# Three-layer decoder block on one core: another order of fills between self-attention and cross-attention, cross-attention two steps sooner, and three waits moved in the feed-forward part

## The chip, the cores and the metric

The kernel runs on one core of one Trainium2 chip. The metric is the device time of one execution in microseconds (us), the median of three runs. The engines are called by their names in the profile: TensorE is PE (its weight loads PEld), VectorE is DVE, ScalarE is ACT, GpSimd is POOL, SyncE, which only issues DMAs here, is SP.

## What is computed

The reference is a post-norm decoder block on x of 8 x 128 x 512 in float32. Its core:

```python
x = layernorm(x + attn(x))      # 32 heads of 16, causal, biases, projections 512 x 512
x = layernorm(x + xattn(x, ctx, ctx, mask))
    # q: 512 -> 32 heads of 128 with rope; k, v: 512 -> 8 heads of 128, k with rope; 4 query heads per kv head
    # out = softmax(q k^T / sqrt(128)) v, then 4096 -> 512
x = layernorm(x + ffn(x))       # gate, up: 512 -> 1376, silu(gate) * up, down: 1376 -> 512
    # their weights are 4-bit codes with a scale and a zero per group of 128 rows
```

Products of float32 are made of float16 halves: a value is split into hi and lo, and each product takes three matmuls (hi x hi, hi x lo, lo x hi). So nearly every tensor is written twice after it leaves a PSUM bank, the hi half by ScalarE (a copy), the lo half by VectorE (value less hi), or both by GpSimd.

## The kernel before, in words

**One list of steps.** The program is one sequence of steps t. Steps 0 to 63 (STEPS1 = 64) are the tiles of the first attention, then a few without attention, and from T0 = 72 on 64 steps v = t - T0 of the cross-attention, until END = 136, and seven more. Every engine walks the same list of steps in its own program with its own order of work within a step, and engines wait for one another through semaphores that count finished tiles. Nothing else orders them.

**First attention, a step t.** TensorE: scores1(t), a projection's part or a fill, weigh1(t - 3) (probabilities by values), turn1(t - 1) (transposes of the probabilities), in every second step turn_out1. VectorE: row_max1(t) (nmax), p1_lo(t - 2) (pT), in every second step normalise, in every eighth turned_out (oTh, oTl). ScalarE: exps1(t) (ebias, prob), p1_hi(t - 1) (pT).

**Fills.** fill_plan (line 61) lists, by hand, extra work of TensorE and the step in which it runs: "o" b, the first attention's output projection of batch b; "t" (0, b), four transposes of its layer norm's result for batch b; "k", "v" and "q" (n, h), projections of the cross-attention's block n (a pair of kv head g and half of the batches, in ORDER). Twelve matmuls of 512 columns make an "o", "k", "q"; 48 of 128 columns a "v". Fill f writes bank f % 2, so it waits until fill f - 2 has been taken out of it (fill_free). Who takes it out (consume, on VectorE): of "k" and "q" rotation_parts (rcos, rsin), then GpSimd's rotation_sum (rot), ScalarE's rotated_hi and GpSimd's rotated_lo one step later; of "v" and "t" ScalarE's values_hi or turned_hi (aTh) and VectorE's values_lo or turned_lo (aTl); of "o" VectorE's add_self and statistics (res, lnst, lnmv), then GpSimd's inverse_sd (lnve, lnrs), and one step later VectorE's apply_norms (res), after which "t" may be made. The first "q" of a half of the batches waits for the four turned tiles of that half. TensorE runs the first fill of a step ahead of weigh, the others behind it.

**Weight splits.** weight_plan (line 123) gives the steps at which the cross-attention's weights of head g are split: QKV_SLOT six pieces, OUT_SLOT four. Those of g = 0 run on GpSimd (split_piece, three instructions), the rest on ScalarE (hi) and, one step later, VectorE (lo). SP loads the next head's weights when the last were split, in program order with its other DMAs.

**Cross-attention, a step v.** TensorE: scores(v), first fill, weigh(v - 2), other fills, merge(v - 3) (output projection into bank 6 or 7). VectorE: add_out(v - 4), row_max(v) (nmax), a weight piece, apply_norms, the first fill if it is "k" or "q", row_sum_inverse(v) (rden), the first fill otherwise, o_lo(v - 2), the other fills. ScalarE: p_hi(v - 1), the first fill's rotated_hi, exps(v), other rotations, weight pieces, o_hi(v - 2), then "v" and "t". GpSimd: p_lo(v - 1), rotated_lo, p_norm(v), rotation_sum. SP turns the probabilities by a DMA transpose (pT<-pn) between p_lo and weigh.

**Gate, up and down.** The inner size is 11 tiles i. Tiles 0 to 3 have split weights; for the first half of the batches they run within the last steps (gate_up(0) to (3)), for the second they are "woven", matmul by matmul, into the coded ones. Tiles 4 to 10 are "coded": 14 items n (a tile and a half of the batches), each multiplying by the raw code differences into 8 banks (four k for gate, m = 0, four for up, m = 1); ScalarE leaves two banks of each m with their scales (leave_bank, left), GpSimd adds them (add_left), VectorE adds the other two (add_bank, total), ScalarE makes the silu, VectorE gated = silu * up, ScalarE inter_hi (inh), GpSimd inter_lo (inl). Then down(b) for each batch b: products over seven tiles (DOWN_SPLIT) with split weights in bank 6 or 7, and down_codes(b) over four (DOWN_CODES) in four other banks, which VectorE scales (scale_part) and GpSimd adds (add_parts).

## Time and profile before

| | |
|---|---|
| median of 3 runs | 903.84 us (903.1 to 905.84) |
| the profiled execution's own time | 903.33 us |
| its span, first to last instruction | 901.5 us |
| mean granted TensorE clock | 0.989 |
| PE busy | 848.8 us (94%) |
| DVE busy | 728.5 us (81%) |
| POOL busy | 571.4 us (63%) |
| ACT busy | 500.4 us (56%) |
| by the chain of work that ended last | PE 49%, DVE 16%, POOL 11%, ACT 10%, issue 9%, DMA 3% |

A row of the timeline is start and length in us, engine, source line, operation, tiles as out<-in, shape and count, and in square brackets the idle time of the engine before it and what ended it. Matmuls are pipelined: a row's length holds a tail of 0.17 us or so, and the pace is seen in the distance of starts. The places of the program in this execution: first attention's step 52 starts at about 158 us, scores(0) at 236, gate/up coded from 764, down from 845 to 895.

### The profile page before, as it was taken

To read this page: it belongs to the slowest core of one execution; us is meant where nothing else is said; L and a number is where in the kernel's file an instruction comes from. 1 tells how busy PE (TensorE), PEld (TensorE's weight loads), DVE (VectorE), ACT (ScalarE), POOL (GpSimd) and SP (SyncE) were. 2 spreads that over 40 slices of the span, in tenths; PEclk is the share of its full clock that TensorE was granted. 3 is DMA by queue.
4 is the path that set the end of the run, shared out by engine and by line. 5 is a ranking of instruction groups with operands and counts; after the bars stand their busy time and mean duration, and the time that the engine had idled before them with its cause. 6 is when DMAs were issued, how large, how long until landed. Compare 5 with 4: busy or idle time off the path is not lost.

```text
span 901.5 us, 17318 instructions
## 1 busy us (share of the span) xinstructions
PE 848.8 (94%) x6141; PEld 471.2 (52%) x6141; DVE 728.5 (81%) x1135; ACT 500.4 (56%) x1493; POOL 571.4 (63%) x504
## 2 busy tenths in 40 slices
PE   8888999889889999999999999999999899899897
PEld 4665777465435555555555555555555444333343
DVE  5589888788857887889788788798799764799887
ACT  4776788563355546646555565554655552777400
POOL 1264439625556766857775667668788642887885
PEclk9999999999989999999999999999999999999999
DMA  6765143420027323224314214222632412230011
GB/s 179 232 196 157 60 141 95 130 94 25 12 36 186 77 55 84 59 71 127 74 24 129 60 36 119 58 36 72 144 69 51 100 30 76 83 122 14 1 47 47
DMA packets 119894, 76.76 MB, mean 85 GB/s; under 512 B 72861, under 2 KB 104064, under 8 KB 119808
## 3 DMA queue, kind: packets, MB, share of 16 engines
q1 hardware_dynamic: 117504, 74.99, 30.9%
q8 instruction: 49, 0.80, 0.4%
q10 hardware_dynamic: 2304, 0.66, 0.3%
q14 instruction: 37, 0.30, 0.1%
HBM read 52.50 MB, written 6.36 MB: 65 GB/s over the span
## 4 chain that ended last, share of the span: by engine, by line
PE 49%; DVE 16%; POOL 11%; ACT 10%; issue 9%; DMA 3%; SPq 0%; ACTq 0%; DVEq 0%; POOLq 0%
PE bank L354 13%; PE bank L355 13%; PE bank L356 13%; POOL rot L623 3%; ACT prob L801 3%; DVE nmax L1085 2%; POOL pn L640 2%; DVE rsin L1164 2%; POOL q2l L629 2%; DVE total L1300 2%; DVE pT L1054 1%; ACT prob L943 1%; POOL deq L652 1%; POOL left L656 1%; ACT pT L752 1%
## 5 line engine op out<-in xcount | busy, mean ns | idle before, releaser
L633 POOL TENSOR_TENSOR prob<-prob,rden 128x512 f32<-128x512 f32 x64 | 66.5, 1039 | 130.5 <-DVE rden L1229 130.5
L623 POOL TENSOR_TENSOR rot<-rcos,rsin 128x512 f32<-128x512 f32 x80 | 106.5, 1331 | 30.7 <-DVE rsin L1164 30.6
L354 PE MATMUL bank<-aTh,xqh 128*128 128x512 f16 x256 | 98.4, 384 | 6.4 <-DVE aTl L1054 4.5
L355 PE MATMUL bank<-aTl,xqh 128*128 128x512 f16 x256 | 98.4, 384 | 0.0
L356 PE MATMUL bank<-aTh,xql 128*128 128x512 f16 x256 | 98.4, 384 | 0.0
L354 PE MATMUL bank<-xoh,o2h 128*128 128x512 f16 x256 | 97.1, 379 | 0.1
L355 PE MATMUL bank<-xol,o2h 128*128 128x512 f16 x256 | 97.1, 379 | 0.0
L356 PE MATMUL bank<-xoh,o2l 128*128 128x512 f16 x256 | 97.1, 379 | 0.0
L943 ACT ACTIVATE prob<-bank,ebias 128x128 f32<-128x128 f32 x256 | 90.4, 365 | 2.1
L752 ACT ACTIVATE ebias<-nmax 128x4 f32<-128x4 f32 x128 | 26.9, 210 | 116.3 <-DVE nmax L1224 75.4
L1164 DVE SCALAR_TENSOR_TENSOR rsin<-bank,sinq 64x512 f32<-64x512 f32 x128 | 88.1, 688 | 1.7
L629 POOL TENSOR_TENSOR q2l<-rot,q2h 128x512 f16<-128x512 f32 x64 | 82.6, 1291 | 5.1 <-ACT q2h L840 5.1
L640 POOL TENSOR_TENSOR pn<-prob,pn 128x512 f16<-128x512 f32 x64 | 81.2, 1269 | 4.1 <-ACT pn L955 4.1
L840 ACT CAST q2h<-rot 128x512 f16<-128x512 f32 x64 | 39.6, 618 | 72.1 <-POOL rot L623 72.1
L955 ACT CAST pn<-prob 128x512 f16<-128x512 f32 x64 | 39.4, 616 | 70.1 <-POOL prob L633 70.1
L801 ACT ACTIVATE prob<-bank,ebias 128x128 f32<-128x128 f32 x256 | 73.0, 368 | 2.2 <-ACT ebias L752 0.2
L1164 DVE SCALAR_TENSOR_TENSOR rcos<-bank,cosq 128x512 f32<-128x512 f32 x64 | 43.8, 684 | 24.6 <-PE bank L356 24.6
L1054 DVE SCALAR_TENSOR_TENSOR o2l<-bank,o2h 128x512 f16<-128x512 f32 x64 | 43.1, 673 | 18.5 <-ACT o2h L752 18.1
L1243 DVE SCALAR_TENSOR_TENSOR res<-bank,res 128x512 f32<-128x512 f32 x64 | 43.9, 686 | 16.4 <-PE bank L356 16.2
L943 ACT ACTIVATION_READ_ACCUMULATOR prob<-bank,ebias 128x1 f32 x256 | 51.9, 203 | 0.0
L1085 DVE TENSOR_REDUCE nmax<-bank 128x4 f32<-128x512 f32 x64 | 43.6, 681 | 9.2 <-PE bank L1531 9.1
L1054 DVE SCALAR_TENSOR_TENSOR pT<-bank,pT 128x512 f16<-128x512 f32 x64 | 43.8, 684 | 8.4 <-ACT pT L752 8.2
(212 smaller groups left out, 2616.8 us busy)
## 6 DMA issues: line engine op xcount, KB each, us to landing
tst<-tables SPq DMA_DIRECT2D x11, 768.0 KB, 5.7
xqs<-in_xwq SPq DMA_DIRECT2D x8, 1024.0 KB, 6.0
xos<-in_xwo SPq DMA_DIRECT2D x8, 1024.0 KB, 5.6
qst<-in_fq SPq DMA_DIRECT2D x11, 384.0 KB, 3.4
kstk<-stack SPq DMA_DIRECT2D x48, 64.0 KB, 2.3
qstk<-stack SPq DMA_DIRECT2D x21, 128.0 KB, 2.6
xs<-in_ctxT SPq DMA_DIRECT2D x2, 1024.0 KB, 7.5
res<-in_x SPq DMA_DIRECT2D x1, 2048.0 KB, 8.3
```

What stands on the lines that cost most here:

```text
L354: pe.matmul(out_ap, ah, bh, start=first, stop=False)
L355: pe.matmul(out_ap, ah, bl, start=False, stop=False)
L356: return pe.matmul(out_ap, al, bh, start=False, stop=last)
L623: nc.gpsimd.tensor_tensor(rot[:, r % 2, :], rcos[:, r % 2, :], rsin[:, r % 2, :], ALU.add).then_inc(rope_rot, 1)
L629: nc.gpsimd.tensor_tensor(lo, rot[:, r % 2, :], hi, ALU.subtract).then_inc(rope_lo, 1)
L633: nc.gpsimd.tensor_tensor(prob[:, v % 2, :].rearrange("p (h k) -> p h k", h=QH), prob[:, v % 2, :].rearrange("p (h k) -> p h k", h=QH), rd ...
L640: nc.gpsimd.tensor_tensor(pn[:, v % 2, 1, :], prob[:, v % 2, :], pn[:, v % 2, 0, :], ALU.subtract).then_inc(c_pn_lo, 1)
L801: last = nc.scalar.activation(prob[:, u % 2, j * S:(j + 1) * S], bank[2 + u % 2][:, j * S:(j + 1) * S], ACT.Exp, bias=ebias[:, u % 2, j:j ...
L943: last = nc.scalar.activation(prob[:, v % 2, j * S:(j + 1) * S], bank[2 + v % 2][:, j * S:(j + 1) * S], ACT.Exp, bias=ebias[:, v % 2, j:j ...
L1054: return nc.vector.scalar_tensor_tensor(out=dst, in0=src, scalar=2.0 ** e, in1=hi, op0=ALU.mult, op1=ALU.subtract)
L1085: nc.vector.tensor_reduce(nmax[:, u % 2, :], bank[2 + u % 2][:, :].rearrange("p (h k) -> p h k", h=4), AX_X, ALU.max, negate=True).then_in ...
L1164: last = nc.vector.scalar_tensor_tensor(out=as_batches(dst[to, r % 2, :]), in0=as_batches(bank[f % 2][src, :]), scalar=2.0 ** (e - E_X - E_W),
```

## The change

T0 is STEPS1 + 6 instead of STEPS1 + 8. The fills of steps 52 to 74 come in another order: k(0) ahead of o(0); each "t" of batches 0 to 3 ahead of the next "o" or "v" in its step; q(0, h) at steps 59 to 62 instead of 61 to 64; k, v, q of block 1 at steps 63 to 69, all of them now ahead of scores(0); o(4) to o(7) in steps T0 and T0 + 1 and t(0,4) to t(0,7) in T0 + 2 and T0 + 3 behind them; block 2's k behind the last "t", its q(0) and q(1) in one step. The splits of head 1's weights close up to steps 54 to 59 (ScalarE, VectorE as before), and GpSimd's pieces 2 and 3 of head 0's output weight go from steps 55 and 58 to 60 and 61. A "t" that is first in its step is now split ahead of the exponentials (ScalarE) and of the row sum's reciprocal (VectorE) in the cross-attention's steps (turned_first); this also holds for t(1,1) and t(1,3) at END - 5 and END - 3. v1's split in the first attention stands ahead of the exponentials (ScalarE) and of pT's (VectorE). SP issues load_q(1) one place sooner. GpSimd's inverse_sds of layer 0 stands at the start of the next step instead of at the end of its own.

In gate/up, inter_hi and inter_lo of item 3 move into the loop of the coded items, behind the first banks of item 4; woven_silu moves ahead of the two banks of up. In down, down_codes(0) runs inside down(0), behind its third tile, and down_codes(1) behind the fifth; down(0) waits for the inl of its own tiles.

```diff
@@ -54,7 +54,7 @@
 ORDER = ([(0, 0), (1, 0), (0, 1), (1, 1)] + [(g, h) for g in range(2, G - 2) for h in range(NHALF)]
          + [(G - 2, 0), (G - 1, 0), (G - 2, 1), (G - 1, 1)])
-T0 = STEPS1 + 8
+T0 = STEPS1 + 6
 IDLE = 16
@@ -64,16 +64,16 @@
-    plan = [(STEPS1 - 12, "o", (0,)), (STEPS1 - 11, "o", (1,)), (STEPS1 - 10, "k", (0,)), (STEPS1 - 10, "t", (0, 0))]
-    plan += [(STEPS1 - 9, "o", (2,)), (STEPS1 - 9, "t", (0, 1)), (STEPS1 - 7, "o", (3,)), (STEPS1 - 7, "t", (0, 2))]
-    plan += [(STEPS1 - 5, "v", (0,)), (STEPS1 - 5, "t", (0, 3))]
-    plan += [(STEPS1 - 3 + h, "q", (0, h)) for h in range(QH)]
-    plan += [(STEPS1 + 1, "k", (1,)), (STEPS1 + 2, "v", (1,))]
-    plan += [(STEPS1 + 3, "q", (1, 0)), (STEPS1 + 4, "q", (1, 1)), (STEPS1 + 5, "q", (1, 2))]
-    plan += [(STEPS1 + 6, "o", (4,)), (STEPS1 + 7, "o", (5,)), (STEPS1 + 7, "o", (6,))]
-    plan += [(T0, "o", (7,)), (T0, "t", (0, 4))]
-    plan += [(T0 + 1, "q", (1, 3)), (T0 + 1, "t", (0, 5)), (T0 + 1, "t", (0, 6)), (T0 + 2, "t", (0, 7))]
-    for block in range(2, len(ORDER)):
+    plan = [(STEPS1 - 12, "k", (0,)), (STEPS1 - 11, "o", (0,)), (STEPS1 - 10, "o", (1,)), (STEPS1 - 9, "t", (0, 0))]
+    plan += [(STEPS1 - 9, "o", (2,)), (STEPS1 - 8, "t", (0, 1)), (STEPS1 - 8, "o", (3,)), (STEPS1 - 7, "t", (0, 2))]
+    plan += [(STEPS1 - 7, "v", (0,)), (STEPS1 - 6, "t", (0, 3))]
+    plan += [(STEPS1 - 5 + h, "q", (0, h)) for h in range(QH)]
+    plan += [(STEPS1 - 1, "k", (1,)), (STEPS1, "v", (1,))]
+    plan += [(STEPS1 + 1, "q", (1, 0)), (STEPS1 + 2, "q", (1, 1)), (STEPS1 + 3, "q", (1, 2)), (STEPS1 + 5, "q", (1, 3))]
+    plan += [(T0, "o", (4,)), (T0, "o", (5,)), (T0 + 1, "o", (6,)), (T0 + 1, "o", (7,))]
+    plan += [(T0 + 2, "t", (0, 4)), (T0 + 2, "t", (0, 5)), (T0 + 3, "t", (0, 6)), (T0 + 3, "t", (0, 7)), (T0 + 3, "k", (2,))]
+    plan += [(T0 + 4, "q", (2, 0)), (T0 + 4, "q", (2, 1)), (T0 + 5, "q", (2, 2)), (T0 + 6, "q", (2, 3)), (T0 + 6, "v", (2,))]
+    for block in range(3, len(ORDER)):
         s = T0 + BH * (block - 1) - 1
@@ -92,6 +92,11 @@
+def turned_first(t):
+
+    return [f for f in fills_at(t)[:1] if FILLS[f][1] == "t"]
+
+
 def find_fill(kind, *what):
@@ -123,8 +128,8 @@
-    qkv = {0: [39, 41, 42, 43, 44, 45], 1: [54, 55, 57, 58, 60, 61]}
-    out = {0: [50, 52, 55, 58], 1: [T0 + 2, T0 + 3, T0 + 4, T0 + 5]}
+    qkv = {0: [39, 41, 42, 43, 44, 45], 1: [54, 55, 56, 57, 58, 59]}
+    out = {0: [50, 52, 60, 61], 1: [T0 + 2, T0 + 3, T0 + 4, T0 + 5]}
     for g in range(2, G):
@@ -522,8 +527,8 @@
             sp.wait_ge(tab_out, 32)
             load_o(0)
+            load_q(1)
             stack_rows(7)
-            load_q(1)
             load_kv(1)
@@ -700,6 +705,7 @@
                 if 0 < j + 1 < BLOCKS and n == 0:
                     split_queries(j + 1)
+                inverse_sds(0, t - 1)
                 pieces(t)
@@ -720,12 +726,11 @@
                     if CODES_SLOT[i] == t:
                         scale_codes(i)
-                inverse_sds(0, t)
                 if t == SCALES_SLOT:
...
                     nc.gpsimd.tensor_copy(scol[:, :, :, :].rearrange("p i m k -> p (i m k)"), scol16[:, :]).then_inc(scol_ready, 1)
                 for n in GU_USE:
-                    if GU_USE[n] == t:
+                    if GU_USE[n] == t and n + 1 < len(GU_USE):
                         inter_lo(n)
@@ -733,8 +738,7 @@
                 if half == 1 and i in DOWN_SPLIT:
                     down_lo(i)
-                if n > len(GU_USE):
-                    inter_lo(n - 1)
+                inter_lo(n - 1)
                 for j in woven_at(n - NSPLIT, 3):
@@ -818,7 +822,7 @@
                 if g == 1:
                     act.wait_ge(v1_psum, BLOCKS)
-                if g >= 2:
+                else:
                     act.wait_ge(fill_psum, last_fill(g - 2) + 1)
@@ -871,8 +875,8 @@
                         rotated_hi(f)
-            def bank_splits(t):
-                for f in fills_at(t):
+            def bank_splits(fills):
+                for f in fills:
                     if FILLS[f][1] == "v":
@@ -907,6 +911,8 @@
                 j, n = t // TILES1, t % TILES1
                 rotations(fills_at(t - 1))
+                if j + 1 < BLOCKS and n == 4 and t > -TILES1:
+                    v1_out(j + 1)
                 if 0 <= t < STEPS1:
@@ -920,8 +926,6 @@
                 if t == FIRST + 5:
                     keep_first_queries()
-                if j + 1 < BLOCKS and n == 4 and t > -TILES1:
-                    v1_out(j + 1)
                 if t == FIRST + TILES1:
@@ -930,7 +934,7 @@
                         x_split_hi(1, k)
                 weight_pieces(t)
-                bank_splits(t)
+                bank_splits(fills_at(t))
@@ -1016,13 +1020,14 @@
                     p_hi(v - 1)
                 rotations(fills_at(t - 1)[:1])
+                bank_splits(turned_first(t))
                 if v < STEPS:
...
                 if 2 <= v <= STEPS + 1:
                     o_hi(v - 2)
-                bank_splits(t)
+                bank_splits([f for f in fills_at(t) if f not in turned_first(t)])
                 if t in LATE_TURN:
@@ -1031,18 +1036,19 @@
                     if GU_USE[n] == t:
                         gate_silu(n)
-                        inter_hi(n)
+                        if n + 1 < len(GU_USE):
+                            inter_hi(n)
             for n in range(len(GU_USE), len(GATE_UP)):
                 i, half = GATE_UP[n]
-                for m in range(2):
-                    for k in range(2):
-                        leave_bank(n, m, k)
-                if n > len(GU_USE):
-                    inter_hi(n - 1)
+                leave_bank(n, 0, 0)
+                leave_bank(n, 0, 1)
+                for j in woven_at(n - NSPLIT, 2):
+                    woven_silu(j)
+                leave_bank(n, 1, 0)
+                leave_bank(n, 1, 1)
+                inter_hi(n - 1)
                 for j in woven_at(n - NSPLIT, 3):
                     woven_hi(j)
-                for j in woven_at(n - NSPLIT, 2):
-                    woven_silu(j)
                 if half == 0 and i in DOWN_SPLIT:
@@ -1343,6 +1349,8 @@
                 if 0 <= t < STEPS1:
                     row_max1(t)
+                if j + 1 < BLOCKS and n == 4 and t > -TILES1:
+                    v1_split_lo(j + 1)
                 if 2 <= t <= STEPS1 + 1:
@@ -1350,8 +1358,6 @@
                     turned_out(j - 1)
                 apply_norms(t)
-                if j + 1 < BLOCKS and n == 4 and t > -TILES1:
-                    v1_split_lo(j + 1)
                 if t in (1, 2, 3):
@@ -1383,13 +1389,13 @@
                 weight_pieces(t - 1)
                 apply_norms(t)
-                turned = [f for f in fills_at(t)[:1] if f in ROPES]
-                for f in turned:
+                early = [f for f in fills_at(t)[:1] if f in ROPES] + turned_first(t)
+                for f in early:
                     consume(f)
...
                     row_sum_inverse(v)
                 for f in fills_at(t)[:1]:
-                    if f not in turned:
+                    if f not in early:
                         consume(f)
@@ -1749,6 +1755,7 @@
             def down(b):
                 if b == 0:
+                    pe.wait_ge(f_ilo, GU_POS[(DOWN_SPLIT[-1], 0)] + 1)
                     pe.wait_ge(f_dlo, NSPLIT)
@@ -1756,7 +1763,9 @@
                     pe.wait_ge(f_y16, b - 1)
                 for k in DOWN_SPLIT:
-                    if k == DOWN_SPLIT[3] and b + 1 < NB:
+                    if k == DOWN_SPLIT[3] and b == 0:
+                        down_codes(0)
+                    if k == DOWN_SPLIT[5 if b == 0 else 3] and b + 1 < NB:
                         down_codes(b + 1)
@@ -1806,7 +1815,6 @@
             for n in range(len(GU_USE), len(GATE_UP)):
                 coded_gate_up(n)
-            down_codes(0)
             for b in range(NB):
```

## Rows read from the trace of the kernel before

**Rows 1.** Windows: core, us, busy us of each engine (instructions), clock, DMA share, GB/s

```profile
158.00:262.00 104.00, 89.96 (x703) 52.28 (x702) 80.01 (x144) 50.44 (x154) 51.30 (x55) 0.93 0.21 62
260.00:690.00 430.00, 427.85 (x2924) 232.12 (x2922) 362.01 (x535) 241.84 (x786) 304.95 (x247) 1.00 0.34 80
```

**Rows 2.** Waits of PE, 158 to 262 us: total, times, longest

```profile
PE bank L354 <- DVE aTl L1054: 4.5, 2, 4.1
PE bank L1607 <- DVE rsin L1164: 2.1, 1, 2.1
PE bank L354 <- DVE v1l L1054: 1.4, 1, 1.4
```

**Rows 3.** Timeline of PE at 174 and at 228 us

```profile
174.48 0.60 PE L354 MATMUL bank<-woTh,oTh 128*128 128x512 f16 x1 [1.92 <-DVE rsin L1164]
174.87 0.63 PE L355 MATMUL bank<-woTl,oTh 128*128 128x512 f16 x1
...
228.44 0.38 PE L354 MATMUL bank<-woTh,oTh 128*128 128x512 f16 x1 [1.10 <-issue]
228.66 0.38 PE L355 MATMUL bank<-woTl,oTh 128*128 128x512 f16 x1
```

**Rows 4.** Windows, one stretch of 2 us

```profile
256.00:258.00 2.00, 2.00 (x6) 0.72 (x5) 0.71 (x2) 1.80 (x10) 0.00 (x0) 0.50 0.68 131
```

**Rows 5.** Gate/up: its window, and one group of DVE's lines

```profile
776.00:838.00 62.00, 58.57 (x262) 24.27 (x261) 58.17 (x73) 45.03 (x75) 51.02 (x41) 1.00 0.20 64
...
L1313 DVE SCALAR_TENSOR_TENSOR gated<-total,gated 128x512 f32<-128x512 f32 x11 | 11.1, 1013 | 0.4
```

**Rows 6.** Timeline of DVE, two row maxima running

```profile
184.67 0.68 DVE L1085 TENSOR_REDUCE nmax<-bank 128x4 f32<-128x512 f32 x1
...
188.90 0.68 DVE L1085 TENSOR_REDUCE nmax<-bank 128x4 f32<-128x512 f32 x1
```

**Rows 7.** Timeline of DVE from 168 to 175 us

```profile
168.71 0.68 DVE L1136 SCALAR_TENSOR_TENSOR res<-bank,res 128x512 f32<-128x512 f32 x1
...
170.25 0.67 DVE L1085 TENSOR_REDUCE nmax<-bank 128x4 f32<-128x512 f32 x1
...
172.33 0.68 DVE L1164 SCALAR_TENSOR_TENSOR rcos<-bank,cosk 128x512 f32<-128x512 f32 x1
...
174.45 0.69 DVE L1054 SCALAR_TENSOR_TENSOR aTl<-bank,aTh 128x512 f16<-128x512 f32 x1
```

**Rows 8.** Timeline of POOL: a weight piece's first part, two rotation sums

```profile
188.53 1.52 POOL L582 TENSOR_SCALAR xos<-xos 128x512 f32<-128x512 f32 x1
...
208.65 1.26 POOL L623 TENSOR_TENSOR rot<-rcos,rsin 128x512 f32<-128x512 f32 x1 [1.06 <-DVE rsin L1164]
...
211.97 1.27 POOL L623 TENSOR_TENSOR rot<-rcos,rsin 128x512 f32<-128x512 f32 x1 [0.17 <-DVE rsin L1164]
```

**Rows 9.** Timeline of DVE at 238 us; one step of the chain

```profile
238.10 0.66 DVE L1224 TENSOR_REDUCE nmax<-bank 128x4 f32<-128x512 f32 x1
...
240.81 0.18 DVE L1229 RECIPROCAL rden<-dens 128x4 f32<-128x4 f32 x1 [0.97 <-ACT dens L752]
...
734.90 3.04 DMA pT<-pn
```

**Rows 10.** Timeline of ACT at 721 us

```profile
721.91 0.59 ACT L752 ACTIVATE aTh<-bank 128x512 f16<-128x512 f32 x1
```

**Rows 11.** Timeline of ACT and of PE at 767 us

```profile
766.50 0.63 ACT L1011 ACTIVATE inh<-gated 128x512 f16<-128x512 f32 x1 [0.86 <-DVE gated L1313]
...
767.76 0.39 PE L1723 MATMUL bank<-aTh,dif 128*128 128x512 f16 x1 [1.52 <-ACT left L982]
```

**Rows 12.** Timeline of PE at 787 us

```profile
787.80 0.38 PE L1709 MATMUL bank<-aTh,wgh 128*128 128x512 f16 x1 [1.37 <-ACT gated_w L1000]
```

**Rows 13.** Timeline of PE and of DVE at the end of gate/up

```profile
844.91 0.39 PE L1747 MATMUL bank<-wdc,inh 128*128 128x512 f16 x1 [2.37 <-POOL inl L662]
...
843.49 0.75 DVE L1300 SCALAR_TENSOR_TENSOR total<-bank,scol,total 128x512 f32<-128x512 f32 x1
```

## Prediction

> **What bounds the kernel now.** I read the sums by stretch first, to see where TensorE is not full, then TensorE's waits there, then the timelines of the engines that end them. In the cross-attention (260 to 690 us) TensorE is busy 427.85 of 430 us: it is the bound, so what is won ahead of 260 us lasts to 690. Between the attentions, 158 to 262 us, it is busy 89.96 of 104 us at a granted clock of 0.93 [rows 1]. The waits there end with VectorE: 4.5 us for aTl (two waits), 2.1 for a rotation, 1.4 for v1l [rows 2]. Behind three of these waits the clock stood at 1.2 instead of 2.4 GHz: matmuls of 512 columns start 0.39 us apart at 174.48, where the same take 0.22 at 228.44 [rows 3], and the window at 256 us shows 0.50 [rows 4]. Yet 158 to 262 is no pure idle time to be had: VectorE works 80.01 us there [rows 1], about TensorE's own work (104 less 14 idle, less the time lost at half clock, some 82). So each step's order decides, not a sum. In gate/up (776 to 838 us) VectorE is busy 58.17 of 62 us [rows 5], TensorE 58.57 with a pipelined tail in each number: both are near full.
>
> **The change, part by part.** Sums are made against the profiled execution: 903.33 us with a span of 901.5. The median of the runs is 903.84, 0.5 above it, and I add that at the end.
>
> *1. Fills of steps 52 to 59.* Removed are two waits: k0 goes first, so that two fills lie between it and the one that needs its bank (the 1.9 us wait that ended at 174.48 [rows 3]); v1's split stands ahead of the softmax pieces on ScalarE and VectorE (1.4 us [rows 2]). What comes instead: now each turned tile comes first in its step and the "o" second. A step with a turned tile has a ring: row maximum on VectorE, exponentials, pT, a weight piece and aTh on ScalarE, aTl on VectorE, next row maximum. Before it takes 4.23 us (184.67 to 188.90 [rows 6]), with "o" worked off inside ScalarE's part. With "o" behind, VectorE takes its addition and statistics after aTl: 1.54 us (168.71 to 170.25 [rows 7]). Steps 55 and 56 so take 5.8 us each, step 57 4.9 (v2l 0.68 behind), and 4.25 more until t(0,3)'s aTl, for which q(0,0) waits: 20.7 us. TensorE has 13.4 us of work in that time (o2, o3, v0 at 2.6 each, four transposes at 0.44, and the first attention's scores, products and turns at 1.25 a step). So it waits some 7.6 us: about 1.5 before each of t(0,1), t(0,2), t(0,3) and 3.2 before q(0,0), plus 0.5 before t(0,0). Walking the engines through from 158 us with these pieces, q(0,0) ends at 195.9 with 2.5 us of first-attention work less behind it than before, where it ends at 200.3: 1.9 us won, at full clock.
>
> *2. Fills of steps 59 to 69.* A rotation costs VectorE 2.1 us (172.33 to 174.45 [rows 7]) under a fill of 2.6; TensorE stays full there. Gone are about 2.2 us of waits (1.1 at 228.44 for oT's last part [rows 3], v2l 0.5, small ones), as q(1,3) now covers oT's last pieces. But the pieces 2 and 3 of the first output weight move from steps 55 and 58, where GpSimd rests, to 60 and 61, where it has a rotation each step. A piece is 1.52 (188.53 [rows 8]) + 0.61 + 1.16, with gaps 3.4 us; sum and remainder of a rotation take 3.3 us a step with ScalarE's cast between them (208.65 to 211.97 [rows 8]). Steps of 3.9 us can't hold 6.7, and GpSimd falls behind by about 3.8 us. ScalarE waits for the rotation's sum ahead of its exponentials, so the exponentials of step 62 end at 213.1 where TensorE's turn wants them at 211.7: 1.4 us lost, and caught up by the v1 step, which has no rotation. This part wins 0.8. The weight splits of VectorE and ScalarE (54 to 59) lie one or two a step under the same fills; their 0.68 us are in the steps above. The four loads on SP: load_q(1) goes ahead of stack_rows(7), whose first wait is later anyway; the load of output weight 1 goes with the last piece to about step 61, needed 11 steps later: nothing.
>
> *3. Steps 70 to 74 (T0 on).* Before, this stretch has the waits of 2.1 and 4.1 us (the latter inside aTl's 4.5 [rows 2]), since t(0,7)'s split stands behind the exponentials and o2's. Now scores(0) starts the softmax two steps sooner, under o4 to o7. From the start of a row maximum to the reciprocal takes 2.71 us (238.10 to 240.81 [rows 9]), then GpSimd's product, the cast, the remainder, and 3.04 us for the turning DMA [rows 9]. On this walk: o6 waits 0.9 us for the addition of o4, which now stands behind the reciprocal; weigh(0) 1.1 us for its DMA; t(0,6) 1.3 us for t(0,4)'s aTl, itself behind two normalisations; weigh(1) 2.4 us for its DMA, since the remainder of p(1) stands behind the inverse deviation of o7; k2 0.6. That is 6.3 us, with small handovers 6.8, in place of 9.8 before (0.6, 2.3, 4.3 from end to start, and 2.7 lost at half clock from 254 to 260): 3.0 won at full clock.
>
> *4. Half clock.* No row shows the clock under the new pattern. A wait of 2.1 us (at 246.93, [rows 2]) left it up; one of 1.9 (at 174.48 [rows 3]), in a step of many small matmuls, was followed by 1.2 GHz. So the bounds are 0 and, with two places (behind q(0,0)'s wait, and behind weigh(1)'s), a fill and a half each: 18 matmuls x 0.2 x 2 = 7 us. The new waits lie close together among scores and transposes, as before 174 and 194 us, so I take both places: 2.0 for the first, 2.9 for the second (as after 254 us). The gains of 1 to 3 are 1.9 + 0.8 + 3.0 = 5.7; less 4.9 this leaves **0.8 us**. What the old half-clock stretches cost is already in the old times.
>
> *5. Softmax order in steps 1 to 51.* v1's split ahead: 0.7 us waits at three steps may go, the exponentials of seven steps start 0.5 later, mostly under a fill. Between -1.3 and +1.5; I take 0.
>
> *6. End of the cross-attention.* turned_first puts aTh and aTl of t(1,1) and t(1,3) ahead of the exponentials. At t(1,1) GpSimd holds the path; nothing. At t(1,3) the 0.59 us of aTh at 721.91 [rows 10] leaves the queue ahead of the gate weights' split and o2's; the chain from there to the wait at 738 us gets **0.5** shorter. Bounds 0 and 0.8; the reverse, if t(1,3) came after its row maximum, is 0.6.
>
> *7. Gate/up.* Leaving the banks of item 4 no longer stands behind inter_hi(3), which waits for VectorE: ScalarE's copy at 766.50 goes behind, and "left" could start at 765.6 instead of 767.03, so TensorE's wait of 1.52 at 767.76 [rows 11] and the first "total" of VectorE come **1.3 us** sooner. Nobody needs inter_hi(3) before item 5's silu, 5 us on. woven_silu ahead of two bank copies takes away three waits like the one of 1.37 us at 787.80 [rows 12], 3 us in all, but VectorE has no idle time over 0.2 us between 775.6 and 837.5: **0**, since it sets the pace there. Bounds 0 and 1.5. VectorE's "gated" takes 1013 ns on average there [rows 5], where the first, at 772.90, takes 690: GpSimd runs beside the later ones. The Trainium skill, "SBUF — State Buffer", section "Who interferes with whom", says that VectorE instructions with two SBUF inputs and GpSimd's reads exclude each other for a whole instruction. By it an order shifted by 1.3 us could hit more or fewer of the eleven, and the sum would lie anywhere from 897.0 (none hit) to about 903.5. The trace agrees as far as the eleven differ (690 to 1460 ns); which ones are hit after the change no row can tell, so it moves no value.
>
> *8. Down.* down(0) starts with three splits products and has down_codes(0) behind them. It waits for the last total of the gate, which VectorE starts at 843.49 for 0.75 us, instead of GpSimd's inl at 844.91 [rows 13]: **0.6 us**. The remainder is ready (844.9) before TensorE gets there (846.2). From there TensorE runs to 895 without a wait.
>
> **Sum**: 0.8 + 0 + 0.5 + 1.3 + 0.6 = 3.2; 903.3 - 3.2 = 900.1, with the median's 0.5: **900.6 us**.
>
> **Rivals.** *A: the clock stays up* (or falls once, short), as at 246.93. Then the transition wins up to 5.7 and all 8.1: 895.5; with 5 and 7 at their good ends 893. For it: no wait is over 3.2 us by my walk, where the worst was 4.1. Against it: there are more of them. *B: the transition wins nothing and part of 6 to 8 is covered*: VectorE's queue (80 us of work for 82) stretches the ring, say 0.4 us in each of 8 steps, and half clock costs its upper 7: 903.3 - 3.2 + 3 = 903 to 905. *C, slower:* the ring of steps 55 to 59 runs at half clock. If the clock falls at the first 1.5 us wait and, since TensorE never fills a stretch after it, stays down through t(0,3) and q(0,0), its 13.4 + 2.6 us of work take 32 and can't hide in 23: +9 instead of 2.0, so 900.6 + 7 = 907.5. It decides from about 12 us of half clock on in that stretch (now 6.8 in two pieces). *D: the change does not act*, since the fills' order is set by the consumers anyway; then 903.8. It can't be whole: part 7 and 8 move instructions past waits that are seen.
>
> **Chances.** Forecast (897.5 to 902.9) 0.50; A 0.20; B and D 0.20; C 0.10. About 0.3% (2.7 us) is what a measurement of this kernel can tell from no change: faster is below 901.1, slower above 906.5. Of the forecast's 0.50, 0.38 lies below 901.1: faster 0.38 + 0.20 = 0.58, same 0.12 + 0.20 = 0.32, slower 0.10. The range 894 to 905 leaves out C and the good tail of A. The likeliest case's own range is 897.5 to 902.9.
>
> **What would show it.** In the changed trace: waits of 1 to 1.5 us before t(0,1) to t(0,3) and one near 3 before the first aT-xq fill; the turn of step 62 waiting for prob; weigh(0) and weigh(1) waiting for the DMA; two stretches of half clock instead of three; "left" right behind silu at 764; three gated_w waits gone with VectorE still above 93%; down starting with inh-wdh products. Wrong would be: a fill that waits longer than 3.5 us, a third half-clock stretch, or waits in steps 1 to 51 that sum to over 3 us more.

## The result, and the profile of the changed kernel

The changed kernel takes 891.97 us (median of 4 runs, 889.28 to 893.17) where the one before takes 904.84 beside it (4 runs, 903.10 to 905.88): ratio 0.9854, 95% interval 0.9833 to 0.9874, so 12.9 us or 1.5% faster. A second comparison gives 891.87 beside 904.20, ratio 0.9855 (0.9831 to 0.9879). Forecast were 900.6 us and a range of 894 to 905: the direction was right, the size (3.2 us) a quarter of what came. The profiled execution took 889.28 us with a span of 887.5, the shortest of its four; against the span of 901.5 of before that is 14.0 us, 1.1 more than the medians give.

Where they lie is best read by laying the two sequences of TensorE's matmuls beside each other and noting how much sooner the same matmul starts. The scores of step 52 are the first such mark (timelines of TensorE, of before and of the changed kernel):

```profile
158.35 0.38 PE L1528 MATMUL bank<-tri,identb 128*128 128x512 bf16 x1
```

```profile
150.80 0.38 PE L1534 MATMUL bank<-tri,identb 128*128 128x512 bf16 x1
```

| mark | before, us | changed, us | sooner by |
|---|---|---|---|
| scores of step 52 | 158.35 | 150.80 | 7.5 |
| v(2), first matmul | 282.79 | 271.56 | 11.2 |
| late product of pT and v2 | 737.99 | 726.46 | 11.5 |
| first wait for "left" in gate/up | 767.76 | 754.74 | 13.0 |
| down, its 32nd matmul | 851.62 | 837.56 | 14.1 |

In down the products come in another order, so the last mark counts matmuls. More than half is won before the first of the moved fills, in steps 1 to 51, where the forecast had put 0. The stretch between the attentions gives 3.7, the end of the cross-attention 0.3, gate/up with down 2.5.

Windows of the changed kernel, which answer to [rows 1] (columns as there), with the same work between the marks:

```profile
150.80:251.90 101.10, 87.58 (x706) 52.51 (x704) 79.78 (x142) 50.13 (x153) 53.01 (x59) 0.97 0.18 53
251.90:680.00 428.10, 425.81 (x2914) 231.37 (x2913) 361.11 (x532) 240.81 (x784) 304.61 (x246) 1.00 0.33 81
```

The cross-attention is as full as it was (425.81 us busy of 428.10). Between the attentions VectorE still works some 80 us, and the granted clock is 0.97 where [rows 1] has 0.93. TensorE's longer waits there (total, times, longest), in place of [rows 2]:

```profile
PE bank L1613 <- DVE aTl L1060: 3.8, 3, 1.4
PE bank L359 <- DVE aTl L1060: 2.9, 1, 2.9
PE bank L359 <- DMA pT<-pn: 2.6, 2, 1.5
PE bank L1546 <- ACT prob L805: 2.2, 2, 1.3
PE bank L1613 <- DVE res L1135: 1.0, 1, 1.0
PE bank L359 <- DVE res L1142: 0.8, 1, 0.8
```

No wait is longer than 2.9 us, where one was 4.1. They are the waits of the forecast's walk (timeline of TensorE; dots stand for rows left out):

```profile
176.55 0.65 PE L1613 MATMUL bank<-ident,res 128*128 128x128 f32 x4 [1.16 <-DVE aTl L1060]
...
187.23 0.38 PE L359 MATMUL bank<-aTh,xqh 128*128 128x512 f16 x1 [2.94 <-DVE aTl L1060]
...
207.04 0.44 PE L1546 MATMUL bank<-ident,prob 128*128 128x128 f32 x2 [1.33 <-ACT prob L805]
...
238.33 0.39 PE L359 MATMUL bank<-pT,v2h 128*128 128x512 f16 x1 [1.04 <-DMA pT<-pn]
241.91 0.66 PE L1613 MATMUL bank<-ident,res 128*128 128x128 f32 x4 [1.44 <-DVE aTl L1060]
244.09 0.61 PE L359 MATMUL bank<-pT,v2h 128*128 128x512 f16 x1 [1.52 <-DMA pT<-pn]
```

In gate/up, TensorE's waits from 750 to 850 us of before:

```profile
PE bank L1709 <- ACT gated_w L1000: 2.7, 3, 1.4
PE bank L1723 <- ACT left L982: 2.4, 3, 1.5
PE bank L1747 <- POOL inl L662: 2.4, 1, 2.4
```

and of the changed kernel:

```profile
PE bank L1729 <- ACT left L986: 2.8, 6, 0.6
PE bank L359 <- DVE total L1306: 1.8, 1, 1.8
```

The wait of 1.52 us for left [rows 11] and the three for gated_w [rows 12] are gone; four of 0.48 us for left have come. Down's first matmul now waits 1.83 us where it waited 2.37 [rows 13], and stands 0.5 us nearer to the last one of gate/up. From the first to the last matmul by code differences ("dif") gate/up takes 77.8 us in all five traces with the old order and 75.8 in all eight with the new: 2.0 won. The group that answers to the last line of [rows 5]:

```profile
L1319 DVE SCALAR_TENSOR_TENSOR gated<-total,gated 128x512 f32<-128x512 f32 x11 | 11.1, 1012 | 0.4
```

Its mean is 1012 ns against 1013: the shifted order left the time of these eleven as it was. The range that the Trainium skill, "SBUF — State Buffer", section "Who interferes with whom", had opened (more or fewer of them hit) was not used: the fourteen "gated" of the whole part sum to 13.26 us before and 13.27 after.

### The profile page after: what moved, and what is told of

Same layout as the page of the kernel before. It is cut to its first block, busy times and chain, and to the rows that moved or that the text cites. A ratio compares the mean times of both kernels' runs of the same rounds, so it can differ in the third digit from the quotient of the medians.

```text
span 887.5 us, 17319 instructions
## 1 busy us (share of the span) xinstructions
PE 840.9 (95%) x6141; PEld 469.5 (53%) x6141; DVE 729.6 (82%) x1135; ACT 500.1 (56%) x1493; POOL 570.5 (64%) x504
## 4 chain that ended last, share of the span: by engine, by line
PE 52%; POOL 15%; DVE 13%; issue 7%; ACT 7%; DMA 4%; SPq 0%; ACTq 0%; POOLq 0%; DVEq 0%
PE bank L359 14%; PE bank L360 14%; PE bank L361 14%; POOL rot L628 3%; DVE total L1306 2%; DMA pT<-pn 2%; POOL pn L645 2%; POOL q2l L634 2%; DVE rsin L1170 1%; ACT prob L805 1%; POOL deq L657 1%; ACT prob L947 1%; PE bank L1546 1%; POOL left L661 1%; DVE nmax L1091 1%
## 5 line engine op out<-in xcount | busy, mean ns | idle before, releaser
L1060 DVE SCALAR_TENSOR_TENSOR o2l<-bank,o2h 128x512 f16<-128x512 f32 x64 | 43.2, 675 | 20.5 <-ACT o2h L756 19.6
```

The source lines that it names most:

```text
L1060: return nc.vector.scalar_tensor_tensor(out=dst, in0=src, scalar=2.0 ** e, in1=hi, op0=ALU.mult, op1=ALU.subtract)
```

## Finding the 7.5 us: seven waits of VectorE

The row that shows them was there before the change: VectorE's v1l, 20 to 200 us, with what the engine waited for in front of it (us, times). First the kernel before, then the changed one:

```profile
L1054 DVE SCALAR_TENSOR_TENSOR v1l<-bank,v1h x7: 690/692/693, 37.8 to 163.5; 128x512 f16<-128x512 f32 x7
its engine sat idle before it (us, times) until:
  ACT v1h L788: 9.1, 7
who waited for it (us, times):
  PE bank L354: 2.8, 3
```

```profile
L1060 DVE SCALAR_TENSOR_TENSOR v1l<-bank,v1h x7: 671/681/692, 35.8 to 152.8; 128x512 f16<-128x512 f32 x7
its engine sat idle before it (us, times) until:
  ACT v1h L792: 1.5, 2
```

9.1 less 1.5 is 7.6 us; one of the seven waits, of 1.07 us at 163.5, lies behind the scores of step 52, so the agreement with the 7.5 us is a rough one. TensorE waited for v1l only 2.8 us in three places, which is all that the forecast had looked at. One such place, VectorE in steps 28 and 29 of before:

```profile
101.99 0.29 DVE L1101 TENSOR_TENSOR onrm<-bank,rden 128x128 f32<-128x128 f32 x1
103.67 0.69 DVE L1054 SCALAR_TENSOR_TENSOR v1l<-bank,v1h 128x512 f16<-128x512 f32 x1 [1.38 <-ACT v1h L788]
104.27 0.68 DVE L1085 TENSOR_REDUCE nmax<-bank 128x4 f32<-128x512 f32 x1
```

and the same work of the changed kernel:

```profile
97.22 0.68 DVE L1091 TENSOR_REDUCE nmax<-bank 128x4 f32<-128x512 f32 x1
97.82 0.68 DVE L1060 SCALAR_TENSOR_TENSOR v1l<-bank,v1h 128x512 f16<-128x512 f32 x1
...
99.25 0.29 DVE L1107 TENSOR_TENSOR onrm<-bank,rden 128x128 f32<-128x128 f32 x1
99.45 0.68 DVE L1091 TENSOR_REDUCE nmax<-bank 128x4 f32<-128x512 f32 x1
```

ScalarE wrote v1h behind exponentials and pT; VectorE stood still for 1.38 us until it came, and the next row maximum, for which ScalarE's next exponentials wait, stood behind it in the same queue. The loss shows on TensorE two to six steps later and in small amounts. These are the scores of steps 30 and 31 (TensorE, before and changed):

```profile
104.06 0.38 PE L1528 MATMUL bank<-tri,identb 128*128 128x512 bf16 x1
107.28 0.38 PE L1528 MATMUL bank<-tri,identb 128*128 128x512 bf16 x1
```

```profile
100.71 0.38 PE L1534 MATMUL bank<-tri,identb 128*128 128x512 bf16 x1
103.33 0.38 PE L1534 MATMUL bank<-tri,identb 128*128 128x512 bf16 x1
```

From one to the other it takes 3.22 us in place of 2.62, and steps 32 to 34 take 0.20, 0.25 and 0.40 more than in the changed kernel. A list of waits hides most of this. TensorE's idle time from step 8 to step 52 is 10.4 us in 36 gaps before and 7.0 in 12 gaps after: 3.4 us less. Each gap costs the tail of the row before it as well, some 0.17 us, and 24 gaps fewer make the other 4.1. The period of the steps, block against block, shows the loss at once.

Over all kernels here it is the same number. From step 8 to step 52 the five traces with the old order of v1's split take 114.7 to 114.9 us, the nine with ScalarE's half of the new order 107.1 to 107.2. The fills, the order of the loads and the place of inverse_sds have no part in it: fills_only below has all of them and takes 114.8. The first two runs test this, the next two the other parts.

*All of part 5 alone*, on the kernel before (VectorE has the same move ahead of p1_lo):

```diff
                 rotations(fills_at(t - 1))
+                if j + 1 < BLOCKS and n == 4 and t > -TILES1:
+                    v1_out(j + 1)
                 if 0 <= t < STEPS1:
                     exps1(t)
```

> The kernel before with one part of the change: v1's split stands ahead of the softmax pieces of its step on ScalarE and VectorE, everything else as before. The trace of the changed kernel reaches the scores of step 52 at 150.80 us where the one before reaches them at 158.35, and before step 52 this order is the only thing that differs in the queues of ScalarE and VectorE. Theory V: that order wins it. VectorE sat idle 9.1 us in seven waits for v1h ahead of v1's remainder in the trace of before, and 1.5 us in two in the changed one; each wait pushed the next row maximum, and with it the softmax of the following steps. Then this kernel reaches step 52 near 151 us and also loses the wait of 1.4 us for v1l at step 54: 904 - 7.5 - 1.5 = 895 us, with 1 us given back to the old fills at most (894.5 to 897). Rival, my recorded estimate for this part: between -1.3 and +1.5 us, taken as 0; then 903 to 905.5, and the 7.5 us come from elsewhere (the start, or the loads' order). Clock: the old stretches at half clock behind the waits of 174 and 194 us stay in both cases.

Measured: 899.34 us beside 905.14, ratio 0.9933 (0.9907 to 0.9958), 6 runs from 893.93 to 900.95. Its trace has step 52 at 150.61 us, 7.7 sooner, and step 54, behind the old wait for v1l, 9.3 sooner, as theory V says. But only 5.8 to 6.1 us arrive in the time, and 899.34 misses the 894.5 to 897 that theory V gave; the next section shows where the rest is.

*Its ScalarE half alone.* The same lines moved on ScalarE, VectorE's v1_split_lo left where it was.

> The kernel before with only the ScalarE half of that order: v1h ahead of the exponentials of its step, v1's remainder left at its old place on VectorE, behind the normalisation. Theory V1 (the cost was the wait of VectorE for v1h): with v1h written earlier the remainder finds it ready wherever it stands, VectorE's idle time of 9.1 us in front of it goes, and this kernel is within 1 us of the one with both halves, near 896. Theory V2 (the place of the remainder in VectorE's queue decides, since it frees the bank of the next fill and keeps 0.69 us away from the next row maximum): less than half of the gain, 899 us or more. Recorded estimate: 0, 903 to 905.

Measured: 897.48 us beside the same 905.14, ratio 0.9921 (0.9901 to 0.9942). In this kernel nothing is left of the wait (VectorE's v1l, its trace):

```profile
L1054 DVE SCALAR_TENSOR_TENSOR v1l<-bank,v1h x7: 680/681/681, 37.2 to 155.7; 128x512 f16<-128x512 f32 x7
its engine sat idle before it (us, times) until:
who waited for it (us, times):
  PEld bank L354: 0.5, 1
```

V1 stands and V2 falls: the whole 7.5 us of steps 8 to 52 come with ScalarE's half, though the remainder stands at its old place in VectorE's queue. What cost was the wait for v1h. Only from step 52 to 54 does VectorE's half add something: 9.25 us before, 8.08 with ScalarE's half, 7.72 with both.

*The rest of the change, without part 5 and without gate/up and down.*

```diff
-T0 = STEPS1 + 8
+T0 = STEPS1 + 6
...
(fill_plan, weight_plan, turned_first, inverse_sds and load_q(1) as changed; v1_out, v1_split_lo, gate/up and down as before)
```

> The changed kernel without the order of v1's split and without the moves in gate/up and down: only the new fills between the attentions, the cross-attention two steps sooner, the weight pieces, turned tiles first, and the order of the loads. From the two traces, shift of the end of v(2) less shift of step 52: 11.2 - 7.5 = 3.7, of which 1.5 belongs to the wait for v1l at step 54 that only the other order removes, and 0.3 more at the end of the cross-attention: 904 - 2.5 = 901.5 us (900 to 903). By my recorded sum: parts 1 to 4 and 6 give 1.3 less that 1.4 of v1l, so 904. By the rival that the clock stays up: 904 - 5.7 - 0.5 + 1.4 = 899. The trace tells the clock term by itself: stretches of half clock between 158 and 262 us, in the order of the recorded two at most, near the first wait of 1 to 1.5 us at the turned tiles and near weigh(1).

Measured: 901.75 us (12 runs), ratio 0.9970 (0.9954 to 0.9985): 2.7 to 3.4 us won, near the 2.5 read from the traces. The part of the gain that is not clock is smaller (next section). Its trace has one stretch of 3.4 us at half clock between the attentions.

*Gate/up and down alone.*

```diff
-                for m in range(2):
-                    for k in range(2):
-                        leave_bank(n, m, k)
-                if n > len(GU_USE):
-                    inter_hi(n - 1)
+                leave_bank(n, 0, 0)
+                leave_bank(n, 0, 1)
+                for j in woven_at(n - NSPLIT, 2):
+                    woven_silu(j)
+                leave_bank(n, 1, 0)
+                leave_bank(n, 1, 1)
+                inter_hi(n - 1)
...
(and inter_lo, and down's start)
```

> The kernel before with only the moves in gate/up and down. Recorded: 1.3 us from the first wait for left, 0 from the three waits for gated_w, 0.6 from down's start: 904 - 1.9 = 902. From the two traces: the shift grows from 11.5 us at 738 us to 14.05 at the start of the last product chain, 2.5 us in all: 901.5. Rival by the order of reads of GpSimd and VectorE in the same memory: anywhere from 900.4 to 904.

Measured: 900.23 us, ratio 0.9949 (0.9931 to 0.9966): 4.6 to 4.9 us, about twice what either reckoning gave (1.9 and 2.5). Its trace has exactly the waits of the changed kernel in gate/up and at down's start, worth 2.0 and 0.5 us, so something else is in the runs' difference: the clock, as the next section shows.

## The clock, run by run

Each run lists its span and its mean granted clock. (1 - clock) x span is what the lower clock could have cost a TensorE that never waits. Over all 132 runs of these kernels, with a level for each kernel and one slope, the span rises by 0.58 us (error 0.04) for each us of it, and single runs lie 0.8 to 0.9 us off. With it each kernel has a span at the same clock, 0.990. These spans are estimates, good to some 0.4 us for a kernel of four to six runs; the one slope is an average, since a fall of the clock costs more in one place than in another, as shown below:

| kernel | median us | median clock | span at clock 0.990 | against before |
|---|---|---|---|---|
| before (49 runs) | 904 to 905 | 0.987 | 901.4 | |
| changed (8 runs) | 891.9 | 0.991 | 890.8 | -10.6 |
| v1_only | 899.34 | 0.984 | 894.4 | -7.0 |
| v1_scalar | 897.48 | 0.986 | 893.9 | -7.5 |
| fills_only | 901.75 | 0.991 | 900.8 | -0.6 |
| ffn_only | 900.23 | 0.9895 | 898.3 | -3.1 |

At one clock the three parts give 7.0 + 0.6 + 3.1 = 10.7 us, the whole 10.6: within the errors they neither help nor hinder each other. The other 2.3 us of the changed kernel go with the clock. By the same table the fills win little at equal clock and some 2 us through the clock; part 5 loses 1 us to it. The one run of v1_only at a clock of 0.992 took 893.93 us, its five others, at 0.983 to 0.985, took 898.74 to 900.95. The comparisons ran on different chips, but the kernel before has the same median clock, 0.987, in each of the three that list it.

The traces show how. A stretch is at half clock where the profile grants 1.2 GHz in place of 2.4 (0.50). In v1_only three stretches of 6.8 us between the attentions stand at half clock, and 3.4 us at 701 and at 841 (windows; the column behind POOL's is the clock):

```profile
165.30:172.10 6.80, 5.45 (x24) 2.15 (x25) 3.95 (x7) 2.57 (x8) 5.19 (x5) 0.50 0.00 2
...
841.20:844.50 3.30, 3.30 (x10) 1.07 (x8) 2.80 (x5) 0.63 (x1) 2.15 (x2) 0.50 0.00 0
```

At step 54 this trace is 9.3 us ahead of the one before, at its end 3.2. In between it holds 27.3 us of half clock where the other holds 13.7; half of the difference is 6.8 us, near the 6.1 that were lost.

Half clock between the attentions, by trace: with the old fills 13.7 us (before), 20.5 (v1_only), 13.7 (v1_scalar), 13.7 (ffn_only), and 13.7 and 10.2 in two kernels below, a mean of 14.2; with the new fills 6.8 and 10.2 (the changed kernel, two executions), 3.4 (fills_only), and 6.8, 10.2, 0, 10.2 and 6.8 in the variants below, a mean of 6.8. The price: in the second execution of the changed kernel the clock is low from 186.4 to 193.3 us, and q(0,0) runs at spacings of 0.43 us,

```profile
187.44 0.58 PE L359 MATMUL bank<-aTh,xqh 128*128 128x512 f16 x1 [2.94 <-DVE aTl L1060]
187.82 0.63 PE L360 MATMUL bank<-aTl,xqh 128*128 128x512 f16 x1
```

where the first had full clock behind the same wait of 2.94 us (187.23 us above; its windows show 1.00 from 188.0 to 194.8). Twelve matmuls so cost 2.5 us. Behind weigh(1) a stretch of 3.4 us costs about 1. And in the first execution of the changed kernel the clock was low in a place that the second ran through at full clock, under o2:

```profile
165.30:168.60 3.30, 3.30 (x24) 2.24 (x23) 3.23 (x7) 1.76 (x7) 0.79 (x2) 0.50 0.01 2
```

It cost 1.1 us there and nothing in the end: the second execution waited 1.25 us ahead of t(0,1), behind o2, and the first did not.

The Trainium skill, "TensorE: Matmul & The Clock Gate", section "Terms", takes the penalty as the time at the lower rate times the share of the clock that is missing; the estimate by it is 3.4 us for 6.8. The trace has 2.5 for q(0,0), as TensorE waits in part of the stretch, and it has nearly all of it at down's start, next.

*Down's start.* In v1_only, v1_scalar and fills_only the stretch at 841 to 844 us begins right behind the start of down (timeline of v1_only):

```profile
840.00 0.39 PE L1747 MATMUL bank<-wdc,inh 128*128 128x512 f16 x1 [2.38 <-POOL inl L662]
...
841.09 0.59 PE L1748 MATMUL bank<-wdc,inl 128*128 128x512 f16 x1
841.47 0.63 PE L1747 MATMUL bank<-wdc,inh 128*128 128x512 f16 x1
```

The profiled execution of before has none there, so nothing warned of it. Down's first 31 matmuls take 6.7 us in it and 8.4 in these three: the stretch costs 1.7 us. The edit, alone on the kernel before:

```diff
                 if b == 0:
+                    pe.wait_ge(f_ilo, GU_POS[(DOWN_SPLIT[-1], 0)] + 1)
                     pe.wait_ge(f_dlo, NSPLIT)
...
-                    if k == DOWN_SPLIT[3] and b + 1 < NB:
+                    if k == DOWN_SPLIT[3] and b == 0:
+                        down_codes(0)
+                    if k == DOWN_SPLIT[5 if b == 0 else 3] and b + 1 < NB:
...
-            down_codes(0)
             for b in range(NB):
                 down(b)
```

> The kernel before with only down's new start (split products first, the coded ones behind the third). Recorded: 0.6 us, since it waits for the last total of VectorE in place of GpSimd's remainder. The traces add this: in the three kernels with the old start that ran beside (v1 order, its ScalarE half, fills) the clock stands at 1.2 GHz for 3.4 us right behind the wait of 2.5 us there; in the six with the new start, whose wait is 2.0 us, it doesn't. Theory: the new start also removes that stretch, about 1.3 us, where it occurs: 904.5 - 0.6 - 1.3 = 902.5. Rival: the stretch depends on gate/up's own waits, not on down's start; then 904, and the stretch shows in this trace near 840.

Measured: 902.80 us (11 runs) beside 904.32, ratio 0.9985 (0.9968 to 1.0001); at clock 0.990 0.8 us less than before. The wait is 1.84 us and the clock is 1.00 from 840 to 850 us:

```profile
840.00:850.00 10.00, 8.16 (x38) 3.57 (x38) 8.14 (x13) 3.62 (x7) 8.50 (x7) 1.00 0.01 2
```

So do all ten traces with the new start, against three of four with the old one that have the stretch. This agrees with the theory; the interval alone (1.4 us, from 2.9 to nothing) does not prove it.

*woven_silu back at its old place*, behind all four bank copies and woven_hi, in the kernel with gate/up and down changed:

```diff
                 leave_bank(n, 0, 1)
-                for j in woven_at(n - NSPLIT, 2):
-                    woven_silu(j)
                 leave_bank(n, 1, 0)
...
                     woven_hi(j)
+                for j in woven_at(n - NSPLIT, 2):
+                    woven_silu(j)
```

> The kernel with only the moves in gate/up and down (900.2 us), with woven_silu back behind all four bank copies and woven_hi. Recorded: the place of woven_silu is worth 0, since VectorE sets the pace of gate/up; then 900.2 within 0.4. From the traces: the three waits for gated_w (1.53, 0.84, 0.76 us) go with the move and three more for left of 0.64 each come: 3.1 less 1.9 = 1.2 us; then 901.4. In its trace the three waits for gated_w come back and those of 0.64 go.

Measured: 901.47 us (11 runs), ratio 0.9968 (0.9955 to 0.9981), 1.2 us slower than ffn_only, which ran in another comparison and whose ratio's interval overlaps, and 1.2 at equal clock (899.5 and 898.3), where each of the two spans is good to 0.3 or so. The waits for gated_w are back:

```profile
PE bank L1709 <- ACT gated_w L999: 2.6, 3, 1.4
PE bank L354 <- DVE total L1300: 1.8, 1, 1.8
PE bank L1723 <- ACT left L981: 0.9, 2, 0.6
```

The traces are finer than the runs: gate/up takes 76.3 us here and 75.8 in ffn_only, so woven_silu is worth 0.5 us. The expectation counted three new waits of 0.64 us for left (0.48 by the rows, and a tail) where there are four: 3.1 less 2.6 is 0.5, not 1.2.

## The waits of the new fills, one at a time

*turned_first taken out of the changed kernel.*

```diff
-    return [f for f in fills_at(t)[:1] if FILLS[f][1] == "t"]
+    return []
```

> The changed kernel with turned_first taken out: the tiles t(0,4), t(0,6), t(1,1), t(1,3) are split behind the exponentials and o2's again. Recorded for the end of the cross-attention: 0.5 us (the wait at 726 us, 1.74 in place of 2.20). At t(0,4) and t(0,6) the split decides the waits before t(0,6) and weigh(1) (1.4 and 1.6 us): behind the exponentials, ScalarE's 1.1 us and more come ahead of it, so 1 to 2 us there. Together 893.5 to 894.5. Rival: these tiles wait for the rows' normalisation anyway, so only the 0.5 at the end: 892.4.

Measured: 898.09 us, ratio 0.9930 (0.9910 to 0.9951): 6.2 us slower than the changed kernel in the other comparisons, 4.4 at equal clock (895.2 and 890.8). That is more than expected, and its trace, 3.1 us longer than that of the changed kernel's second execution, shows why:

```profile
245.19 1.12 PE L1613 MATMUL bank<-ident,res 128*128 128x128 f32 x4 [3.30 <-DVE aTl L1060]
251.22 0.39 PE L359 MATMUL bank<-cTh,xkh 128*128 128x512 f16 x1 [2.84 <-DVE aTl L1060]
```

t(0,6) waits 3.30 us in place of 1.44, and k2 waits 2.84 for the last tile's split where it waited 0 or 0.6; part of the matmuls between run at half clock (the transposes take 1.12 in place of 0.66). At the end the wait before the late product is 2.04 again in place of 1.58 (2.20 and 1.74 by the distance of starts), the forecast's 0.5.

*The output projection ahead of the tile again in steps 55 and 56.*

```diff
-... (STEPS1 - 9, "t", (0, 0))]
-    plan += [(STEPS1 - 9, "o", (2,)), (STEPS1 - 8, "t", (0, 1)), (STEPS1 - 8, "o", (3,)), ...
+    plan += [(STEPS1 - 9, "o", (2,)), (STEPS1 - 9, "t", (0, 0)), (STEPS1 - 8, "o", (3,)), (STEPS1 - 8, "t", (0, 1)), ...
```

> The changed kernel with the output projection ahead of the turned tile again in steps 55 and 56 (t(0,0) moves into step 55 behind o2, t(0,1) stays in 56 behind o3). Theory of the prediction: behind the tile, the addition and the statistics of o cost VectorE 1.54 us inside the ring of each of these steps; ahead of it they lie inside ScalarE's part. Then these two steps take 4.3 us in place of 5 to 5.7, the wait of 3.1 us before q(0,0) falls below 1, and the kernel takes 889 to 890 us. Rival: the ring is set elsewhere (each tile waits for its normalised rows, and those for the addition of o two steps earlier), and the wait only moves to the tiles: 892 within 1. Other side: with the order of before, the wait ahead of a rotation or of aTl comes back (2.1 us and a stretch at half clock): 893.5 to 895.

Measured: 891.02 us beside 891.87 of the changed kernel in the same comparison, ratio to before 0.9848 (0.9828 to 0.9868); at equal clock 889.4 against 890.8. Of the 2 to 3 us expected, 1.4 came at equal clock, and the rival's range holds the median: the wait before q(0,0) is still 2.94 us, and one of the two projections now waits 1.06 us for the addition of an earlier one on VectorE (L1142), close to what the rival said. From row maximum to row maximum step 55 takes 4.36 us in place of 5.76, step 56 takes 5.33: the ring was shortened as reckoned once and not twice, as it has more than one bound.

*Two pieces of the output weight back at steps 55 and 58.*

```diff
-    out = {0: [50, 52, 60, 61], ...
+    out = {0: [50, 52, 55, 58], ...
```

> The changed kernel with the third and fourth piece of the first output weight at steps 55 and 58 on GpSimd, as before the change, in place of 60 and 61. Theory of the prediction: at 60 and 61 they push GpSimd's rotation and so the exponentials of step 62; the wait of 1.5 us for prob at 207 us in the changed trace is theirs, and goes: 890.5 us. Rival: at 55 and 58 GpSimd's 3.4 us a piece run beside VectorE in the ring of the turned tiles, which is the bound there, and lengthen VectorE's instructions by what the wait gives: 892 within 0.7.

Measured: 891.10 us, ratio to before 0.9847 (0.9823 to 0.9871); 889.8 at equal clock, 1.0 won, about the size of the error; the trace is the better witness. The wait of 1.33 us for prob in step 62 is gone, the waits at the tiles are the same to 0.05 us. So GpSimd's pieces set it, and no wait has grown with them at 55 and 58.

*v(0) behind t(0,3).*

```diff
-    plan += [(STEPS1 - 7, "v", (0,)), (STEPS1 - 6, "t", (0, 3))]
+    plan += [(STEPS1 - 6, "t", (0, 3)), (STEPS1 - 6, "v", (0,))]
```

> The changed kernel with v(0) one step later, behind t(0,3), in place of behind t(0,2). Theory: TensorE waits 3.1 us for aTl of t(0,3) before q(0,0) with nothing to do; v(0) is 2.6 us of work that can stand there, and its split (0.7 us on VectorE) leaves the ring ahead of t(0,3). The ring of steps 55 to 58 shortens by 0.7, the wait before q(0,0) falls to about 0.5, and the kernel takes 891 us. Rival: TensorE's wait only moves ahead of t(0,3), and v's split on ScalarE and VectorE now stands ahead of the first rotation, so nothing or +0.7: 892 to 893.

Measured: 889.96 us, ratio to before 0.9839 (0.9819 to 0.9859); 0.9 us less than the changed kernel at equal clock, and the rest by the clock. The wait of 2.94 us is split into 0.98 before v(0) and 1.03 before q(0,0), that before t(0,3), which follows sooner now, is 1.41, and the whole stretch runs at full clock in this execution:

```profile
160.00:262.00 102.00, 87.15 (x704) 51.38 (x703) 81.38 (x144) 51.00 (x156) 51.78 (x56) 1.00 0.20 55
```

*The three together.*

> The changed kernel with the three variations of the last runs together: the output projection ahead of the turned tile in steps 55 and 56, the first output weight's third and fourth piece at steps 55 and 58, v(0) behind t(0,3). Alone they gave 891.0, 891.1 and 890.0 beside 891.9 of the changed kernel. If they act at different waits (1.0 and 1.3 us at the tiles, 1.3 at step 62, 2 of the 3.0 before q(0,0)), they add: 888 to 889 us, with at most one stretch at half clock between the attentions. Rival: the pieces on GpSimd at 55 and 58 and the additions meet in VectorE's queue, and it stays at 890.

Measured: 887.35 us (886.13 to 887.84) beside 904.32 of before, ratio 0.9811 (0.9792 to 0.9829): the fastest kernel here, 4.5 us below the changed one, though measured on another chip. At equal clock it is 3.5 below, where the sum is 1.4 + 1.0 + 0.9 = 3.3, so within the errors they add. In its trace no wait before q(0,0) is left. At most one stretch at half clock was expected and the trace has two, of 3.4 us each; in the median its clock, 0.9945, is still the highest of all.

The changed kernel once more, in the same comparison as the three variants, as their base:

> The changed kernel again, beside the next three, which are variants of it. Expected: 892 us within 1.5, mean clock 0.990 to 0.993. It serves as the base of their comparison, with span and clock of each run.

Measured: 891.87 us (890.89 to 892.84), clocks 0.991 to 0.994.

## Where the prediction held and where it failed

**Part 5, softmax order, is the step that failed**: forecast 0 with bounds of -1.3 and +1.5, measured 7.5 us between steps 8 and 52 in every trace. The run with this part alone wins 7.0 at equal clock (5.8 to 6.1 by the medians), and that includes the 1.4 of the v1l wait of step 54, which the forecast had in its part 1; the traces have the two at 9.3. It priced the order by TensorE's few waits for v1l. VectorE's own idle time of 9.1 us in front of v1l was never asked for. The engine was busy 0.86 to 0.90 of the time from 58 to 148 us and looked as if it had room, but row maximum, exponentials and pT form a chain from step to step, and an idle 1.38 us inside it cost 1.3 to 1.5 us in each of the last four blocks, as the periods show. The test named in the forecast, waits in steps 1 to 51 that sum to over 3 us more, looked only for a loss; the waits of TensorE fell by 3.4 us, less than half of what was won.

**Parts 1 to 3, the walk of the new waits, held**, mostly to 0.3 us: 1.5 at the tiles was 1.2, 0.5 before t(0,0) was 1.0, 3.2 before q(0,0) was 2.9, 1.4 in step 62 was 1.3, 0.9 at o6 was 0.8, 1.1 at weigh(0) was 1.0, 1.3 at t(0,6) was 1.4, 0.6 at k2 was 0 and 0.6; only weigh(1), 2.4, was far off with 1.5. The ring itself was right: 5.8, 5.8, 4.9 and 4.25 us were forecast, and VectorE's row maxima lie 5.76, 5.76, 4.82 and 4.23 apart in the second execution. But what was summed as "won at full clock" was measured against an old stretch that held 13.7 us of half clock, whose loss went into the gain. At equal clock the fills win 0.6 us.

**Part 4, the clock, was mis-sized**: 4.9 us for the new pattern. The second execution of the changed kernel has both of its places, and the falls cost 2.5 and about 1 us, not 2.0 and 2.9. The profiled one has only the second; its first fall, at 165.3 us, is at a place that the forecast did not name, and the wait behind it took the cost back. So the forecast of two stretches instead of three came true there in number, but by luck: one of them was another. With 6.8 us of half clock on average in place of 14.2, the clock was the gain of the fills and not their loss.

**Part 6** was right at the end of the cross-attention (0.5). What turned_first is worth at t(0,4) and t(0,6), some 3 to 4 us, was hidden in the walk of part 3 and had no price of its own.

**Part 7**: 1.3 for left was right (1.5). woven_silu, forecast 0, is worth 0.5. The argument was that VectorE has no idle time over 0.2 us and so sets the pace, and most of it held: TensorE's three waits for gated_w, 2.7 us, gave way to four of 0.48 for left.

**Part 8**: 0.6 was right (0.5 by the traces), but for a stretch at half clock behind the old wait, 1.7 us, that three of four old traces have and the profiled one had not. It fits the surplus of ffn_only.

By the two profiled executions the miss is 10.8 us (14.0 less 3.2): 7.5 of part 5, 2.9 of parts 1 to 4 (3.7 less 0.8), 0.6 of parts 7 and 8 (2.5 less 1.9), less 0.2 of part 6 (0.3 where 0.5 was forecast). The medians of the runs give 1.1 less, since this execution was the fastest of its four. Of the rivals, A ("the clock stays up", 895.5; its own sum gives 895.7) came nearest, for a reason that covers a quarter of the miss. C did not occur: no trace of the new fills has the ring at half clock for more than 6.8 us. What stays open is when the clock falls: the same wait of 2.94 us was followed by half clock in one execution of the same kernel and not in another.

## What to carry to other kernels

Where several engines pass a chain from step to step, ask each of them for its own idle time in front of every instruction of the chain, not only TensorE for its waits: the loss of a step comes out on TensorE spread over the next ones, in gaps too short for a list. Compare the periods of like steps; here one of them was 0.6 us longer in block after block, two steps behind the culprit. And take the span together with the clock of several executions before a gain is put down to an order: the single profiled one may lack a stretch at half clock that most others have, or hold one that they lack.

## What the hardware showed

The mean clock of one and the same kernel, the one before, varied from 0.983 to 0.992 between runs, and its time from 901.3 to 908.4 us with it; a part that wins 7 us of order can show 6 because more of its work then falls into half clock (v1_only, 0.984). A stretch of 3.4 us cost 1.7 us at down's start, where TensorE never waits in it, about 1 behind weigh(1), and nothing where a wait followed that took it back; one of 6.8 us cost 2.5 at q(0,0).
